# Router logits by column groups, and the mixing blocks as one product with a mask

## The chip, the cores and the metric

One core of one Trainium2 chip runs the whole layer as one program. The metric is the device time of an execution in microseconds (us). The core has a matrix engine (TensorE, PE in the rows; the loading of its stationary operand is PEld), a vector engine (VectorE, DVE), an activation engine (ScalarE, ACT), a general one (GpSimd, POOL), and a queue engine (SyncE, SP) that issues most DMAs. TensorE reads SBUF and writes PSUM (eight banks of 512 fp32 per partition). Each engine runs its instructions in order and waits on semaphores.

## The reference, cut to what matters

```python
# x: (64, 32, 512); cond: (64, 128)
h = gelu(cond @ W0 + b0); h = gelu(h @ W1 + b1)
att = softmax(h @ W2 + b2)                         # (64, 8)
agg_w = einsum('bk,koi->boi', att, weight)         # a 32x32 matrix for each batch row
agg_b = att @ bias_k
xt = einsum('boi,bih->boh', agg_w, x) + agg_b      # mixing; 2048 tokens of 512
logits = xt @ router_w + router_b                  # 512 -> 16 experts
scores = softmax(logits) + router_bias             # best 2 of 4 groups, best 2 experts in them
y = sum over experts of gate * ((silu(xt @ w1 + b1) * (xt @ w2 + b2)) @ w3 + b3)
z = (silu(xt @ sw1 + sb1) * (xt @ sw2 + sb2)) @ sw3 + sb3
out = x + y + z
```

## The kernel before

The 2048 tokens are 16 tiles of 128 (NT = 16), four tiles make a group of 512 columns (GT = 4, NG = 4), and a tile holds four batch rows of 32 channels (BPT = 4). The width of 512 is four chunks of 128 (C = 4).

**Start.** TensorE makes the conditioning in small products with warming products between them (`keep_warm`, products of the identity that nobody reads). The last, with `is_block`, puts `att` of every tile into PSUM bank 5, spread over partitions.

**Mixing stage.** VectorE's `mix(first, end)` builds the stationary matrices `mixT` of one or two tiles: it multiplies `mix_w` by `att` (L946), adds over the eight kernels (L972), copies the bias column (L974), and copies four 32x32 blocks per tile onto the diagonal of a zeroed 128x128 matrix in SBUF (L977, four copies of 32 partitions). Three calls stand at the start; later ones stand behind every second copy of a transposed tile. In step s of TensorE's loop (L605 to L631) stand the product that mixes tile s (512 columns, fp32), the four transposes of tile s-1 (L621), and the logits of tile s-2: four products with a 128x128 block of `xT` as the stationary operand and 16 columns of the router's weights as the moving one. An fp32 product is two instructions in the rows, a transpose is one. ScalarE evicts the mixed tile to a ring of four buffers (L825), from which SP stores it to HBM; VectorE copies the transposed tile to `xT` (L987). ScalarE and GpSimd split tiles into a rounded part and a rest (L835, L457).

**Behind it.** TensorE runs the first half of the shared expert (`shared_up`) without a break, while VectorE works on the routing from the logits: scores, the two best experts, `chosen`; then TensorE counts ranks with two products on `chosen` (`ranks_done`), VectorE makes slots and codes from them, and the dispatch product (32 products, `codes_ready`, `pool_codes`) makes the tables by which GpSimd gathers token rows. The experts' loop follows, then the shared expert's second half and the sums.

What sets the order is the program as written, engine by engine, with semaphores. Of importance below: `mix_copied` (VectorE to TensorE), `xt_ready` (ScalarE to TensorE and SP), `xT_ready` (VectorE to TensorE and ScalarE), `xt_stored` (a store has landed, ring buffer free), `logits_done` (TensorE to VectorE), `chosen_ready`, `ranks_done`.

## Time and profile before

| what | us |
|---|---|
| median of 3 runs | 261.38 |
| lowest and highest | 259.18, 262.07 |
| the profiled execution | 260.76 |
| its span, first to last instruction | 258.9 |
| mean granted TensorE clock, share of full | 0.993 |

The profiled execution is 1.86 us longer than its span. All times in the rows are from the span's start. In a row of the timeline stand: start, time from the first start to the last end, engine, line of the program, operation, out<-in, shapes, xcount, and in brackets the idle time before it with what ended it.

### The profile page before, as it was taken

To read this page: it belongs to the slowest core of one execution; us is meant where nothing else is said; L and a number is where in the kernel's file an instruction comes from. 1 tells how busy PE (TensorE), PEld (TensorE's weight loads), DVE (VectorE), ACT (ScalarE), POOL (GpSimd) and SP (SyncE) were. 2 spreads that over 40 slices of the span, in tenths; PEclk is the share of its full clock that TensorE was granted. 3 is DMA by queue.
4 is the path that set the end of the run, shared out by engine and by line. 5 is a ranking of instruction groups with operands and counts; after the bars stand their busy time and mean duration, and the time that the engine had idled before them with its cause. 6 is when DMAs were issued, how large, how long until landed. Compare 5 with 4: busy or idle time off the path is not lost.

```text
span 258.9 us, 4022 instructions
## 1 busy us (share of the span) xinstructions
PE 241.5 (93%) x1092; PEld 162.9 (63%) x1093; DVE 149.7 (58%) x314; ACT 78.7 (30%) x169; POOL 111.8 (43%) x135
## 2 busy tenths in 40 slices
PE   7847988999999889999999999999999999999695
PEld 6715756788875346667777777777777744444241
DVE  0599899649979977434333333333444401498982
ACT  2223535413147100333343333333333321111300
POOL 7782455410020344456666666666665321000720
PEclk9999999999999999999999999999999999999979
DMA  6998686697326938954555444455444224999853
GB/s 199 341 416 326 249 302 240 248 321 294 142 101 253 425 114 242 363 175 156 173 171 163 130 150 156 133 166 167 169 168 139 84 86 171 396 387 387 322 191 134
DMA packets 20699, 57.91 MB, mean 224 GB/s; under 512 B 2533, under 2 KB 2533, under 8 KB 20428
## 3 DMA queue, kind: packets, MB, share of 16 engines
q1 hardware_dynamic: 15084, 39.89, 42.2%
q0 software_dynamic: 5600, 17.83, 20.8%
q8 instruction: 7, 0.11, 0.2%
q14 instruction: 8, 0.07, 0.1%
HBM read 40.94 MB, written 17.30 MB: 225 GB/s over the span
## 4 chain that ended last, share of the span: by engine, by line
PE 81%; DVE 13%; DMA 3%; issue 2%; ACT 0%; DVEq 0%
PE psum L578 72%; PE psum L724 6%; DVE r L977 4%; DVE xT L1207 3%; DVE xT L972 2%; DVE xT L946 2%; DVE xT L987 2%; PE psum L621 2%; PE psum L737 2%; DMA late_region<-xt_rows,from_row 1%; DMA xT<-cond_pack 1%; DVE mix_bias L974 0%; ACT late_region L842 0%; DVE r L1163 0%; DVEq L1166 0%
## 5 line engine op out<-in xcount | busy, mean ns | idle before, releaser
L578 PE MATMUL psum<-wexp,r 128*128 x272 | 68.5, 381 | 0.3 <-DVE r L1163 0.2
L578 PEld LDWEIGHTS psum<-wexp,r 128*128 128x128 f32 x272 | 48.4, 190 | 22.8 <-issue 16.9
L946 DVE TENSOR_TENSOR r<-psum,ebias 128x256 f32<-128x256 f32 x34 | 14.4, 424 | 64.2 <-PE psum L578 64.2
L490 POOL DMA_INDIRECT late_region<-xt_rows,from_row x36 | 35.6, 990 | 23.9 <-issue 16.6
L496 POOL DMA_INDIRECT expert_rows<-late_region,to_row x33 | 33.3, 1010 | 26.8 <-issue 18.3
L578 PE MATMUL psum<-wexp,xt_sb 128*128 x68 | 34.8, 594 | 0.0
L883 ACT ACTIVATE r<-r 128x128 f32<-128x128 f32 x34 | 10.5, 310 | 57.6 <-DVE r L946 57.6
L578 PE MATMUL psum<-xT,shared_sb 128*128 128x512 f32 x64 | 28.0, 594 | 0.0
L889 ACT ACTIVATE late_region<-psum 128x512 f32<-128x512 f32 x34 | 20.3, 598 | 13.9 <-PE psum L578 13.9
L1163 DVE COPY r<-psum 128x512 f32<-128x512 f32 x36 | 24.5, 679 | 0.0
L724 PE MATMUL psum<-ident,late_region 128*128 128x128 f32 x144 | 21.6, 273 | 1.0 <-DMA late_region<-xt_rows,from_row 1.0
L578 PE MATMUL psum<-x_split,w_split 128*128 128x512 f32 x96 | 22.3, 392 | 0.0
L578 PEld LDWEIGHTS psum<-xT,shared_sb 128*128 128x128 f32 x64 | 12.0, 190 | 15.5 <-issue 14.6
L724 PEld LDWEIGHTS psum<-ident,late_region 128*128 128x128 f32 x144 | 17.9, 141 | 5.5 <-issue 2.0
L578 PEld LDWEIGHTS psum<-x_split,w_split 128*128 128x128 f32 x96 | 17.9, 188 | 3.7
L578 PE MATMUL psum<-router_sb,xT 128*128 128x16 f32 x128 | 15.8, 256 | 3.3 <-DVE xT L987 3.3
L825 ACT ACTIVATE xt_sb<-psum,mix_bias 128x512 f32<-128x512 f32 x16 | 11.0, 687 | 25.8 <-PE psum L578 15.8
L578 PEld LDWEIGHTS psum<-router_sb,xT 128*128 128x128 f32 x128 | 15.5, 192 | 4.1 <-DVE xT L987 4.0
L457 POOL TENSOR_TENSOR x_split<-xT,x_split 128x512 fp32r<-128x512 f32 x8 | 10.2, 1279 | 12.3 <-ACT x_split L835 12.3
L571 POOL TENSOR_TENSOR xt_sb<-xt_sb,wexp 128x512 f32<-128x512 f32 x2 | 3.3, 1663 | 27.1 <-ACT wexp L933 27.1
L987 DVE COPY xT<-psum 128x512 f32<-128x512 f32 x16 | 10.8, 689 | 5.8 <-PE psum L621 5.6
L879 ACT ACTIVATE xt_sb<-psum 128x128 f32<-128x128 f32 x34 | 9.4, 278 | 15.2 <-PE psum L737 15.2
(175 smaller groups left out, 311.0 us busy)
## 6 DMA issues: line engine op xcount, KB each, us to landing
wexp<-expert_pack SPq DMA_DIRECT2D x16, 768.0 KB, 5.3
wexp<-expert_rows SPq DMA_DIRECT2D x8, 1024.0 KB, 12.8
xt_rows<-xt_sb SPq DMA_DIRECT2D x16, 256.0 KB, 2.8
x_early<-x SPq DMA_DIRECT2D x2, 1024.0 KB, 8.1
late_region<-x SPq DMA_DIRECT2D x2, 1024.0 KB, 12.7
ebias<-expert_bias SPq DMA_DIRECT2D x1, 2048.0 KB, 7.1
out_dram<-x_early SPq DMA_DIRECT2D x8, 256.0 KB, 9.7
shared_sb<-shared_pack SPq DMA_DIRECT2D x1, 1536.0 KB, 16.4
```

Of the source, the lines that this page charges most:

```text
L457: T.tensor_tensor(rest, whole, part, ALU.subtract).then_inc(split_ready, 1)
L490: nc.gpsimd.indirect_dma_start(out=xg[:, slot, :], out_offset=None, in_=xt_dram[:, :], in_offset=bass.IndirectOffsetOnAxis(ap=index.bitcas ...
L496: nc.gpsimd.indirect_dma_start(out=y_dram[:, :], out_offset=bass.IndirectOffsetOnAxis(ap=index.bitcast(U32), axis=0), in_=y_sb[:, slot, :] ...
L578: return nc.tensor.matmul(dst, lhsT, rhs, start=start, stop=stop)
L724: last = nc.tensor.transpose(psum[:, b, c * P:(c + 1) * P], xg[:, slot, c * P:(c + 1) * P], ident[:, :])
L825: nc.scalar.activation(xt_ring[:, t % RING, :], psum[:, t % 2, :], ACT.Identity, bias=mix_bias[:, t:t + 1]).then_inc(xt_ready, 1)
L883: nc.scalar.activation(s_sb[:, b, :], h_sb[:, b, 0, :], ACT.Silu).then_inc(s_ready, 1)
L889: nc.scalar.activation(y_sb[:, slot, :], psum[:, 6 + b, :], ACT.Copy).then_inc(y_ready, 1)
L946: return nc.vector.tensor_tensor(dst, a, b, op)
L977: last = V.tensor_copy(mixT[rows, first:end, b * IN_C:(b + 1) * IN_C], mix_sum[rows, 0:T, 0:IN_C])
L987: V.tensor_copy(xT[:, t // GT, :, (t % GT) * P:(t % GT + 1) * P], psum[:, 2 + t % 2, :].rearrange("p (c n) -> p c n", c=C)).then_inc(xT_re ...
L1163: V.tensor_copy(xgT[:, b], psum[:, b, :].rearrange("p (c n) -> p c n", c=C)).then_inc(xgT_ready, 1)
```

## The change

Four edits, beside names.

1. **Block mask.** The four block copies and the bias copy in `mix` become one product: the summed rows, repeated four times along the free axis, times a mask of 128x4 that lies in PSUM bank 5 behind `att`. TensorE puts the mask there once, as identity times `in_block`; GpSimd makes `in_block` instead of zeroing `r1`. The sums live in a part of `wexp` that is loaded later, and ScalarE takes its bias from there.
2. **Logits by column groups.** Instead of 16 x 4 products with 16 moving columns there are, per group of four tiles, four products with 512 moving columns: chunk c of the router's weights (16 columns padded to 32 with zeros, `rw_wide`) is stationary in 32 columns of the array, and its result goes to partitions 32c to 32c+31 of one PSUM bank. ScalarE copies that bank to SBUF (`logits_copied`), and four products with `chunk_sum` (the identity folded to 16 columns, so that the four chunks are added) turn it back to token rows (`logits_to_rows`).
3. **Place of the last group.** The rows of the last group are made behind the first six products of `shared_up`, so `logits_done` comes there. SP's load of `ebias`, on whose space `rw_wide` and `chunk_sum` lie, now waits for `logits_done` too.
4. **Warming.** `keep_warm(8)` before the `is_block` product becomes `keep_warm(4)`.

TensorE's order in the mixing loop (in the names `x_early,r` is the mixing product, `ident,xt_sb` the transposes, `router_sb,xT` the logits). Before, steps 5 and 6:

```order
L578 MATMUL psum<-x_early,r 128x512 [waits xt_ready,mix_copied]
L621 MATMUL psum<-ident,xt_sb 128x128 [waits xT_ready,xt_ready]
L621 MATMUL psum<-ident,xt_sb 128x128 x3
L578 MATMUL psum<-router_sb,xT 128x16 [waits xT_ready]
L578 MATMUL psum<-router_sb,xT 128x16 x3
L578 MATMUL psum<-x_early,r 128x512 [waits xt_ready,mix_copied]
L621 MATMUL psum<-ident,xt_sb 128x128 [waits xT_ready,xt_ready]
L621 MATMUL psum<-ident,xt_sb 128x128 x3
L578 MATMUL psum<-router_sb,xT 128x16 [waits xT_ready]
L578 MATMUL psum<-router_sb,xT 128x16 x3
```

The same two steps now (`xT,ebias` are the column-group products, `ebias,r` the turning back):

```order
L590 MATMUL psum<-x_early,r 128x512 [waits xt_ready,mix_copied]
L651 MATMUL psum<-ident,xt_sb 128x128 [waits xT_ready,xt_ready]
L651 MATMUL psum<-ident,xt_sb 128x128 x3
L590 MATMUL psum<-xT,ebias 32x512 [waits rw_ready,xT_ready]
L590 MATMUL psum<-xT,ebias 32x512 x3
L590 MATMUL psum<-x_early,r 128x512 [waits xt_ready,mix_copied]
L651 MATMUL psum<-ident,xt_sb 128x128 [waits xT_ready,xt_ready]
L651 MATMUL psum<-ident,xt_sb 128x128 x3
L590 MATMUL psum<-ebias,r 128x16 [waits logitsT_ready]
L590 MATMUL psum<-ebias,r 128x16 x3
```

The two steps that follow hold no logits at all; the pattern repeats with steps 9 and 10, and 13 and 14.

VectorE, the mix of two tiles and the copies behind it, before:

```order
L946 TENSOR_TENSOR xT<-xT,psum 128x528
L972 TENSOR_REDUCE xT<-xT 128x66 [waits dve_chain]
L974 COPY mix_bias<-xT 128x2 [waits dve_chain]
L977 COPY r<-xT 32x2x32 x4
L987 COPY xT<-psum 128x4x128 [waits xtT_done] x2
```

And now:

```order
L980 TENSOR_TENSOR xT<-xT,psum 128x528
L1010 TENSOR_REDUCE wexp<-xT 128x66 [waits dve_chain]
L980 TENSOR_TENSOR r<-wexp,psum 128x256 [waits dve_chain]
L1024 COPY xT<-psum 128x4x128 [waits xtT_done] x2
```

Five copies became one product that reads the mask from PSUM; the copies of transposed tiles keep their places.

```diff
@@ -137,7 +137,6 @@
         mix_terms = early(P, 2 * KMIX * (IN_C + 1)).rearrange("p (t k o) -> p t k o", t=2, k=KMIX)
-        mix_sum = early(P, 2 * (IN_C + 1)).rearrange("p (t o) -> p t o", t=2)
         gateT = xT[0:GROWS, 0, :, :].rearrange("p c n -> p (c n)")[:, 0:TOKENS // 2].bitcast(BF16)
@@ -153,6 +152,10 @@
         wexp_flat = wexp[:, :, :].rearrange("p e n -> p (e n)")
+        mix_rows = wexp[:, E - 1, 0:NT * (IN_C + 1)].rearrange("p (t o) -> p t o", t=NT)
+        rw_wide = ebias_flat[:, 4 * DIM:4 * DIM + C * IN_C].rearrange("p (c e) -> p c e", c=C)
+        chunk_sum = ebias_flat[:, 4 * DIM + C * IN_C:4 * DIM + C * IN_C + E]
+        logitsT = [r1[:, q * GN:(q + 1) * GN] for q in (0, 1, 2, 1)]
         rows_k = wexp_flat[:, 0:NG * TOPK * GT * DIM].rearrange("p (g k t d) -> p g k t d", g=NG, k=TOPK, t=GT)
@@ -171,7 +174,7 @@
         sb12_sb = router_sb[:, C * E + 2 * E:].rearrange("p (w i) -> p w i", w=2)
-        mix_bias = sb("mix_bias", [P, NT])
+        in_block = sb("in_block", [P, BPT])
         rev_e = sb("rev_e", [P, E])
@@ -209,7 +212,7 @@
         masks_ready = sem("masks_ready")
-        blocks_zeroed = sem("blocks_zeroed")
+        in_block_ready = sem("in_block_ready")
         ident_bf_ready = sem("ident_bf_ready")
@@ -219,6 +222,9 @@
         mix_copied = sem("mix_copied")
+        rw_ready = sem("rw_ready")
+        logitsT_done = sem("logitsT_done")
+        logitsT_ready = sem("logitsT_ready")
         xt_done = sem("xt_done")
@@ -352,6 +358,7 @@
             sp.wait_ge(b3_ready, 1)
+            sp.wait_ge(logits_done, 1)
             sp.dma_start(ebias_flat, expert_bias.to_broadcast([P, E * 2 * INTER])).then_inc(half_loaded[0], 16)
@@ -404,7 +411,12 @@
                                     ).then_inc(masks_ready, 1)
-            nc.gpsimd.memset(r1[:, :], 0.0).then_inc(blocks_zeroed, 1)
+            link(nc.gpsimd.memset(in_block[:, :], 1.0))
+            link(nc.gpsimd.affine_select(out=in_block[:, :], in_=in_block[:, :], compare_op=ALU.is_ge, fill=0.0,
+                                         base=0, pattern=[[-IN_C, BPT]], channel_multiplier=1))
+            nc.gpsimd.affine_select(out=in_block[:, :], in_=in_block[:, :], compare_op=ALU.is_ge, fill=0.0,
+                                    base=IN_C - 1, pattern=[[IN_C, BPT]], channel_multiplier=-1
+                                    ).then_inc(in_block_ready, 1)
             link(nc.gpsimd.memset(ones_bf[:, :], 1.0))
@@ -593,14 +605,32 @@
             mm(psum[0:BS, 4, 0:KMIX], h2T, W2_sb).then_inc(pe_cond, 1)
-            keep_warm(8)
+            keep_warm(4)
             pe.wait_ge(masks_ready, 1)
             pe.wait_ge(dve_cond, 2)
             mm(psum[:, 5, 0:NT * KMIX], is_block.rearrange("b r i -> b (r i)"),
                att_spread.rearrange("b t k -> b (t k)")).then_inc(pe_cond, 1)
+            pe.wait_ge(in_block_ready, 1)
+            mm(psum[:, 5, NT * KMIX:NT * KMIX + BPT], ident[:, :], in_block[:, :]).then_inc(pe_cond, 1)
             keep_warm(8)
+
+            def logits_by_chunk(g):
+
+                if g == 0:
+                    pe.wait_ge(rw_ready, 1)
+                for c in range(C):
+                    last = mm(psum[c * IN_C:(c + 1) * IN_C, 6 + g % 2, :], rw_wide[:, c, :], xT[:, g, c, :])
+                last.then_inc(logitsT_done, 1)
+
+            def logits_to_rows(g):
+                pe.wait_ge(logitsT_ready, g + 1)
+                for t in range(g * GT, (g + 1) * GT):
+                    cols = slice((t % GT) * P, (t % GT + 1) * P)
+                    last = mm(psum[:, 4, t * E:(t + 1) * E], logitsT[g][:, cols], chunk_sum)
+                if g == NG - 1:
+                    last.then_inc(logits_done, 1)
@@ -621,15 +651,11 @@
                     last.then_inc(xtT_done, 1)
-                if s >= 2:
-                    t = s - 2
-                    if t == 0:
-                        pe.wait_ge(router_loaded, 16)
-                    pe.wait_ge(xT_ready, t + 1)
-                    for c in range(C):
-                        last = mm(psum[:, 4, t * E:(t + 1) * E], xT_tile(t, c), rw_sb[:, c, :],
-                                  start=(c == 0), stop=(c == C - 1))
-            last.then_inc(logits_done, 1)
+                if s >= GT + 1 and (s - 1) % GT == 0:
+                    pe.wait_ge(xT_ready, s - 1)
+                    logits_by_chunk(s // GT - 1)
+                if s >= GT + 2 and (s - 2) % GT == 0:
+                    logits_to_rows(s // GT - 1)
@@ -678,7 +704,7 @@
             pe.wait_ge(split_ready, SPLITS)
-            shared_up(0, 0)
+            shared_up(0, 0, between={(0, 1): lambda: logits_to_rows(NG - 1)})
             shared_up(0, 1)
@@ -816,6 +842,11 @@
             nc.scalar.activation(att_e, att, ACT.Exp, accum_out=att_sum).then_inc(act_cond, 1)
+
+            def logits_copied(g):
+                act.wait_ge(logitsT_done, g + 1)
+                nc.scalar.activation(logitsT[g], psum[:, 6 + g % 2, :], ACT.Copy).then_inc(logitsT_ready, 1)
+
             for t in range(NT):
@@ -823,7 +854,9 @@
                 nc.scalar.activation(xt_ring[:, t % RING, :], psum[:, t % 2, :], ACT.Identity,
-                                     bias=mix_bias[:, t:t + 1]).then_inc(xt_ready, 1)
+                                     bias=mix_rows[:, t, IN_C:IN_C + 1]).then_inc(xt_ready, 1)
+                if t >= GT + 1 and (t - 1) % GT == 0:
+                    logits_copied(t // GT - 1)
@@ -833,6 +866,7 @@
                     nc.scalar.activation(part, whole, ACT.Copy).then_inc(part_ready, 1)
+            logits_copied(NG - 1)
             act.wait_ge(shifted_ready, 1)
@@ -947,6 +981,9 @@
+            link(V.memset(rw_wide, 0.0))
+            dve.wait_ge(ident_ready, 1)
+            V.tensor_reduce(chunk_sum, ident[:, :].rearrange("p (c e) -> p e c", c=C)[:, 0:E, :], AX_X, ALU.add)
             dve.wait_ge(pe_cond, 3)
@@ -959,8 +996,9 @@
                                    op0=ALU.mult, op1=ALU.mult).then_inc(dve_cond, 1)
-            dve.wait_ge(pe_cond, 4)
-            dve.wait_ge(blocks_zeroed, 1)
+            dve.wait_ge(router_loaded, 16)
+            V.tensor_copy(rw_wide[:, :, 0:E], rw_sb).then_inc(rw_ready, 1)
+            dve.wait_ge(pe_cond, 5)
@@ -969,14 +1007,13 @@
                         att_here.unsqueeze(3).to_broadcast([P, T, KMIX, IN_C + 1]), ALU.mult))
-                link(V.tensor_reduce(mix_sum[:, 0:T], mix_terms[:, 0:T].rearrange("p t k o -> p t o k"),
+                link(V.tensor_reduce(mix_rows[:, first:end], mix_terms[:, 0:T].rearrange("p t k o -> p t o k"),
                                      AX_X, ALU.add))
-                V.tensor_copy(mix_bias[:, first:end], mix_sum[:, 0:T, IN_C])
-                for b in range(BPT):
-                    rows = slice(b * IN_C, (b + 1) * IN_C)
-                    last = V.tensor_copy(mixT[rows, first:end, b * IN_C:(b + 1) * IN_C],
-                                         mix_sum[rows, 0:T, 0:IN_C])
-                last.then_inc(mix_copied, 1)
+                shape = [P, T, BPT, IN_C]
+                tt(mixT[:, first:end].rearrange("p t (b o) -> p t b o", b=BPT),
+                   mix_rows[:, first:end, 0:IN_C].unsqueeze(2).to_broadcast(shape),
+                   psum[:, 5, NT * KMIX:NT * KMIX + BPT].unsqueeze(1).unsqueeze(3).to_broadcast(shape), ALU.mult
+                   ).then_inc(mix_copied, 1)
             for step in range(3):
                 mix(*MIXES[step])
```

## Rows read from the trace of the kernel before

**Rows 1.** The page: the chain that ended last by line, and one costly group.
```profile
PE psum L578 72%; PE psum L724 6%; DVE r L977 4%; DVE xT L1207 3%; DVE xT L972 2%; DVE xT L946 2%; DVE xT L987 2%; PE psum L621 2%; PE psum L737 2%; DMA late_region<-xt_rows,from_row 1%; DMA xT<-cond_pack 1%; DVE mix_bias L974 0%; ACT late_region L842 0%; DVE r L1163 0%; DVEq L1166 0%
...
L825 ACT ACTIVATE xt_sb<-psum,mix_bias 128x512 f32<-128x512 f32 x16 | 11.0, 687 | 25.8 <-PE psum L578 15.8
```
**Rows 2.** Stretches: length, PE, PEld, DVE, ACT, POOL busy, granted clock, DMA share, GB/s.
```profile
12.90:25.50 12.60, 7.33 (x36) 4.47 (x37) 12.10 (x25) 3.90 (x6) 6.99 (x8) 1.00 1.01 381
25.50:35.40 9.90, 9.04 (x59) 6.69 (x58) 8.90 (x19) 4.93 (x8) 5.12 (x5) 1.00 0.70 253
...
56.40:89.70 33.30, 33.15 (x141) 23.18 (x140) 29.51 (x63) 11.93 (x24) 4.41 (x6) 1.00 0.63 246
246.00:250.00 4.00, 3.97 (x6) 1.65 (x7) 4.00 (x7) 0.00 (x0) 1.51 (x2) 0.59 0.71 262
```
**Rows 3.** Timeline of TensorE, start and mixing stage.
```profile
7.47 0.38 PE L578 MATMUL psum<-xT 128*64 128x8 f32 x2
7.79 2.05 PE L578 MATMUL psum<-ident 128*128 128x128 f32 x16
9.77 0.48 PE L578 MATMUL psum<-xT 64*128 64x128 f32 x2
...
13.03 1.10 PE L578 MATMUL psum<-x_early,r 128*128 128x512 f32 x2 [0.80 <-DVE r L977]
...
19.29 1.12 PE L578 MATMUL psum<-x_early,r 128*128 128x512 f32 x2 [2.17 <-DVE r L977]
...
29.88 1.10 PE L578 MATMUL psum<-x_early,r 128*128 128x512 f32 x2
30.82 0.60 PE L621 MATMUL psum<-ident,xt_sb 128*128 128x128 f32 x4
31.26 0.96 PE L578 MATMUL psum<-router_sb,xT 128*128 128x16 f32 x8
...
34.48 1.06 PE L578 MATMUL psum<-router_sb,xT 128*128 128x16 f32 x8 [0.86 <-DVE xT L987]
```
**Rows 4.** Timeline of VectorE, mixes of one tile and of two.
```profile
9.06 0.35 DVE L959 SCALAR_TENSOR_TENSOR xT<-xT 64x128 f32<-64x128 f32 x1
10.29 0.43 DVE L946 TENSOR_TENSOR xT<-xT,psum 128x264 f32<-128x264 f32 x1 [0.89 <-PE psum L578]
10.76 0.63 DVE L972 TENSOR_REDUCE xT<-xT 128x33 f32<-128x264 f32 x1
...
15.54 0.70 DVE L946 TENSOR_TENSOR xT<-xT,psum 128x528 f32<-128x528 f32 x1
16.27 1.10 DVE L972 TENSOR_REDUCE xT<-xT 128x66 f32<-128x528 f32 x1
...
17.48 1.75 DVE L977 COPY r<-xT 32x64 f32<-32x64 f32 x4
19.27 0.69 DVE L987 COPY xT<-psum 128x512 f32<-128x512 f32 x1
...
27.12 0.78 DVE L977 COPY r<-xT 32x64 f32<-32x64 f32 x4
```
**Rows 5.** DMA issues between 14.9 and 15.5 us: KB, us to landing.
```profile
xt_rows<-xt_sb SPq DMA_DIRECT2D x1, 256.0 KB, 6.9
```
**Rows 6.** Timeline behind the mixing stage: TensorE, VectorE, GpSimd.
```profile
56.40 16.62 PE L578 MATMUL psum<-x_split,w_split 128*128 128x512 f32 x72
...
90.39 1.52 PE L578 MATMUL psum<-r,late_region 128*128 128x96 bf16 x32 [0.73 <-issue]
...
56.58 0.42 DVE L946 TENSOR_TENSOR late_region<-psum,router_sb 128x256 f32<-128x256 f32 x1 [1.16 <-PE psum L578]
...
73.29 0.42 DVE L1079 COPY late_region<-psum 128x256 f32<-128x256 f32 x1 [1.44 <-PE psum L578]
...
88.23 2.06 POOL L473 TENSOR_TENSOR r<-r,hi_code 128x480 bf16<-128x480 bf16 x1 [11.57 <-DVE r L1116]
```
**Rows 7.** Timeline of TensorE, the shared expert's second half.
```profile
211.14 25.05 PE L578 MATMUL psum<-xT,shared_sb 128*128 128x512 f32 x58
```

## The prediction

> **What bounds the kernel now.** I read the chain of waits first: TensorE's products end last, and the largest parts that are not TensorE are VectorE's block copies (L977) and the rest of the mix, all in the first 56 us [rows 1]. So the stretches come next. From 12.9 to 25.5 us VectorE is busy 12.10 of 12.60 us and TensorE 7.33: VectorE sets the pace. From 25.5 to 35.4, one group of four tiles, TensorE is busy 9.04 of 9.90 us and waits once, 0.86 us, for a copy of a transposed tile that stands behind a mix. From 56.4 to 89.7 TensorE is busy 33.15 of 33.30 [rows 2, 3]. The edits lie in the first two stretches; what they win or lose there is the time at which `shared_up` starts (S, now 56.40 [rows 6]), and what they add behind S counts by itself.
>
> **Start.** VectorE has `att_spread` at 9.41 (9.06 + 0.35 [rows 4]), but TensorE's product on it starts at 9.77, behind sixteen warming instructions from 7.79 on [rows 3]. Eight end near 8.8, so the product can start at 9.5; the mask's product adds some 0.2 behind it, and VectorE's first mix starts at 10.2 instead of 10.29. The copy of the router's weights on VectorE fits in its 0.89 us of idle time before that. The granted clock was 1.00, the 2.4 GHz level, through the 2.17 us in which TensorE waited before 19.29 [rows 2, 3], so I cost four fewer warming products at nothing.
>
> **The mix.** A product of VectorE with a PSUM operand took 0.43 us for 264 elements and 0.70 for 528, about 1.02 ns each; the block product of 256 is then 0.42, of 128 0.29. It takes the place of four copies in 1.75 us (0.78 in some mixes) and a bias copy [rows 4]. A mix of two tiles becomes 0.70 + 1.10 + 0.42 and gaps = 2.32 us, of one tile 1.46. From 10.2 the three first mixes end at 11.66, 13.12 and 15.44; the third mixing product, now at 19.29 [rows 3], can start at 15.5: **3.8 us won early**. Most of that reaches the first column-group products. They wait for VectorE's copy of tile 3 (15.44 + 0.72 + 2.32 + 1.32 + 2.32 + 0.69 = 22.8), and for the transposes of tile 4, whose eviction needs the store of tile 0. That store, issued at 14.9, lands 6.9 us later, at 21.8 [rows 5], behind loads in the same queue, and an earlier issue does not change that; with the eviction (0.69 [rows 1]) and the transposes TensorE is at 23.06.
>
> **The logits.** A mixing product with its transposes takes 1.38 us from start to start (29.88 to 31.26), eight instructions of old logits 0.81 (0.96 less the 0.15 by which the shown ends lag) [rows 3]. Call c the time of the four column-group products of a group. The turning back is again eight instructions with 16 columns, 0.81. A period is then four times 1.38, c, 0.81, and a wait: VectorE's copy of tile 6 starts 0.66 behind its transposes, a mix and the copy of tile 7 follow, so that copy ends 0.66 + 0.72 + 2.32 + 0.69 = 4.39 later, where TensorE is ready after 3.19; with the semaphore 1.26 us. Period 7.59 + c, against 9.90 now: even at c = 2.3. The last stretch has two mixing products, three sets of transposes, one turning back and waits of 1.5 us: 5.51 + c. So S = 23.06 + 2 x 7.59 + 5.51 + 4c = 43.75 + 4c. The same walk over the kernel before gives 55.95 where the trace has 56.40, so I add 0.45: **S = 44.2 + 4c**.
>
> ScalarE gains four copies of 512 columns (0.69 as its evictions [rows 1]), hidden: TensorE needs each only behind a mixing product and a set of transposes (1.38 us), or behind six products (1.4). GpSimd loses the zeroing and gains three small operations, off the path.
>
> **The value of c.** No row shows column groups. A 512-column fp32 product is two instructions of 0.43 us (25.05 us for 58 [rows 7]). If nothing overlaps, c = 8 x 0.43 = 3.44; if all four columns run side by side, 0.86. I take the middle case. The two instructions of one product use the same 32 columns and cannot overlap each other; instructions start in the order of the program; so each product's second half runs beside the next one's first: five slots, 2.15 us. Going to narrow columns and back costs something: the 128x64 product took 0.32 us to the next start for a pair, where a full-width pair of 16 columns takes 0.20, and the 64x128 pair took 0.48, where a full-width pair of 128 columns takes 2.05 / 8 = 0.26 [rows 3]; bounds 0 and 0.35, I take 0.25 since going in is partly hidden in the 1.26 us wait. **c = 2.4.** The Trainium skill speaks against free switching: TensorEngine Tiling (Array Packing), Key Properties, says that a change of the tiling mode drains the engine. The rows on the two odd-shaped products agree in sign, and the sum has the 0.25 either way.
>
> **Behind S.** The last turning back now stands in `shared_up`: +0.81 on TensorE. `logits_done` comes 1.39 (six products) + 0.81 + 0.15 = 2.35 us behind S, where VectorE now starts 0.18 behind it. VectorE's later start of 2.17 is covered as far as the counts: it waits 1.44 us there for TensorE, and TensorE comes 0.81 later itself, 2.25 in all [rows 6]. From there on both are 0.81 late, and the dispatch (which starts 90.39, when GpSimd's codes end at 88.23 + 2.06 [rows 6]) follows. The load of `ebias` starts some 2 us later behind S; its reader stands beyond 100 us. I count 0.9.
>
> **Sum.** 44.2 + 4c - 56.4 + 0.9 = 4c - 11.3; with c = 2.4, -1.7 us. The profiled execution took 260.76, so **259.1 us**. That execution is 0.62 below the median of the runs shown, 261.38. Without switching cost -2.7 (258.1), with 0.35 -1.3 (259.5).
>
> **Rival 1: all four columns overlap.** c = 0.86 + 0.25 = 1.1, net -6.9, **253.9 us**. For it: four different parts of the array and of PSUM, and only one semaphore per group. Against: the order of the halves above, which no row can prove. The Trainium skill, TensorE: Matmul & The Clock Gate, Part 3 (Packing small matmuls), reports 2.38 times for three column tiles and starts a few ns apart; its span rule would give this case. The same part says that products start and end strictly in order, by which the second half of each would hold up the next, as I forecast. No run here shows it yet.
>
> **Rival 2: the column groups run one after another** (slower). Where each fp32 product streams 512 columns alone, c = 3.44 + 0.25 = 3.7, net +3.5, **264.3 us**. Place: TensorE at the end of each group; it decides from c = 2.83 on, where the sum is zero. For it: every 512-column product in the trace goes at 0.43 per instruction, whatever its content, and the old form needed 3.26 per group. Against: the output partitions put each product into its own 32 columns.
>
> **Rival 3: the routing starts too late.** Cover for `logits_done` is 2.25 against 2.17 needed. If ScalarE's last copy or the turning back comes 1 to 2 us later than worked out, VectorE's routing and the dispatch are late by that, and the result is 260 to 261.5, no change.
>
> Worth noting for any outcome: by the same walk the mask alone, with the old logits, would put S at 49.1, 7.3 earlier. The column groups pay only if c is near 1; at c = 2.4 they give back over four us of what the mask wins.
>
> **Numbers.** Chances: forecast 0.50, rival 1 0.15, rival 2 0.23, rival 3 0.12. About 1%, 2.6 us, can be told from no change; the three runs before spread by 2.9. Part of that may be the clock: behind a wait near 246 us the granted clock was 0.59 on average over 4 us [rows 2], between the two levels, and a shift of the whole end can move that by up to 1.8 us either way. Faster by over 1%: rival 1, and 0.4 of the forecast (low c, or the clock): 0.36 with a little of rival 3. Slower by over 1%: most of rival 2, and 0.04 of mishaps in the routing: 0.20. Within 1%: 0.44. The range reaches from rival 1 to just short of rival 2: 253.3 to 264.0; the forecast's own is 258.0 to 260.0.
>
> **What the profile after would show.** Right: the third mixing product near 15.5; one VectorE product of 0.42 us per pair of tiles and no 32-row copies; the first column-group products near 23; 2.4 us from the first of four to the next mixing product; `shared_up` near 53.8; the dispatch 34.9 us behind that. Wrong: starts of the four products 0.9 apart (rival 2) or all within a short time (rival 1), a VectorE wait that no longer stands before the counts (rival 3), or a block product that takes as long as the copies did.

## The result and the profile after

The changed kernel took **250.95 us** (median of 4 runs, 250.71 to 251.96) beside 260.56 us for the kernel before on the same chip: a ratio of 0.965 [0.961, 0.970]. The prediction was 259.1 with a range from 253.3 to 264.0, so it was wrong: right in sign, far too small. The profiled execution took 250.74 us, its span is 249.0, the granted clock 0.991. Medians here are over all executions of a kernel; a ratio leaves out those over 1.5% above their kernel's fastest, among them one of 489.55 us of the kernel with all stores first and one of 418.35 us of the kernel before.

Where the two profiled executions stand at the same points (us from the span's start):

| point | before | after | difference |
|---|---|---|---|
| third mixing product | 19.29 | 14.78 | -4.51 |
| `shared_up` begins (S) | 56.40 | 49.38 | -7.02 |
| dispatch begins | 90.39 | 84.32 | -6.07 |
| second half of the shared expert begins | 207.52 | 200.97 | -6.55 |
| last product of TensorE ends | 255.70 | 245.44 | -10.26 |
| span | 258.9 | 249.0 | -9.9 |

So there are two gains, some 6 to 7 us in the mixing stage and 3.7 us in the last 48 us. The second was in no term of the prediction's sum.

The page's chain of waits, which answers to [rows 1]: the block copies are gone from it, and the store of a tile (`xt_rows<-xt_sb`, 4% of the span) is new.
```profile
PE psum L590 69%; PE psum L750 6%; DMA xt_rows<-xt_sb 4%; DVE xT L1244 3%; DVE xT L980 2%; PE psum L651 2%; PE psum L763 2%; DVE xT L1024 1%; DMA xT<-cond_pack 1%; DVE xt_sb L1244 1%; DVE x_early L980 1%; DVE wexp L1010 1%; ACT xt_sb L856 1%; DVE xt_sb L980 1%; ACT L844 1%
```
The timeline of VectorE, where the first mixes were in [rows 4]: product, sum, and now one block product with a PSUM operand, 0.29 us for a tile and 0.42 for two.
```profile
9.79 0.43 DVE L980 TENSOR_TENSOR xT<-xT,psum 128x264 f32<-128x264 f32 x1 [0.85 <-PE psum L590]
10.25 0.63 DVE L1010 TENSOR_REDUCE wexp<-xT 128x33 f32<-128x264 f32 x1
10.92 0.29 DVE L980 TENSOR_TENSOR r<-wexp,psum 128x128 f32<-128x128 f32 x1
...
12.44 0.70 DVE L980 TENSOR_TENSOR xT<-xT,psum 128x528 f32<-128x528 f32 x1
13.17 1.10 DVE L1010 TENSOR_REDUCE wexp<-xT 128x66 f32<-128x528 f32 x1
14.31 0.42 DVE L980 TENSOR_TENSOR r<-wexp,psum 128x256 f32<-128x256 f32 x1
```
The timeline of TensorE, beside [rows 3]. `psum<-xT,ebias` with 128*32 are the four column products of a group (eight instructions); the number in brackets is the wait before them.
```profile
14.78 1.13 PE L590 MATMUL psum<-x_early,r 128*128 128x512 f32 x2 [0.64 <-DVE r L980]
...
19.03 1.02 PE L590 MATMUL psum<-x_early,r 128*128 128x512 f32 x2
23.11 1.12 PE L651 MATMUL psum<-ident,xt_sb 128*128 128x128 f32 x4 [3.05 <-ACT xt_sb L856]
24.15 1.94 PE L590 MATMUL psum<-xT,ebias 128*32 128x512 f32 x8
26.02 1.19 PE L590 MATMUL psum<-x_early,r 128*128 128x512 f32 x2
...
33.44 1.06 PE L590 MATMUL psum<-xT,ebias 128*32 128x512 f32 x8 [1.01 <-DVE xT L1024]
34.44 1.12 PE L590 MATMUL psum<-late_region,r 128*128 128x512 f32 x2
...
49.38 1.67 PE L590 MATMUL psum<-x_split,w_split 128*128 128x512 f32 x6
```
From start to next start a group's four products take 1.00 us (33.44 to 34.44), where the prediction had 2.4. The first group took 1.87, and the four transposes ahead of it 1.04 instead of some 0.5. The stretches around them, columns as in [rows 2], show why: the granted clock was 0.50, the 1.2 GHz level, behind the 3.05 us in which TensorE waited.
```profile
19.00:24.00 5.00, 1.95 (x8) 0.94 (x6) 2.49 (x4) 1.63 (x3) 2.93 (x4) 0.88 1.00 403
24.00:26.00 2.00, 2.00 (x10) 0.20 (x8) 1.70 (x3) 0.15 (x1) 0.92 (x1) 0.50 1.03 421
```
That wait comes from a store. ScalarE's timeline shows that its eviction of tile 4 waited for the store of tile 0 to land, and the issue row of that store gives 8.9 us where [rows 5] had 6.9. SP issued it at 13.31, before at 14.94: so it landed at 22.2 and before at 21.8, nearly the same time in spite of the earlier issue.
```profile
22.37 0.69 ACT L856 ACTIVATE xt_sb<-psum,wexp 128x512 f32<-128x512 f32 x1 [3.54 <-DMA xt_rows<-xt_sb]
```
```profile
xt_rows<-xt_sb SPq DMA_DIRECT2D x1, 256.0 KB, 8.9
```
How eight instructions fit into 1.00 us is read by cutting the timeline: up to 33.88 TensorE has begun four of the eight, and all eight have begun by 33.92.
```profile
33.44 0.64 PE L590 MATMUL psum<-xT,ebias 128*32 128x512 f32 x4 [1.01 <-DVE xT L1024]
```
So four halves begin together at 33.44 and the other four 0.45 us later: two slots, not five. The rows do not name the columns; that the first four are the first halves of the four products is argued, since the two halves of one product use the same columns.

**The end.** GpSimd adds the four tiles of the last group; VectorE's additions of the third group (L1207 before, L1244 after) have two operands in SBUF. Before, GpSimd starts just ahead of VectorE's last two: these take some 1.75 us each instead of 0.74, all eight 7.53 us, and TensorE waits 2.08 us and then runs slowly. The timelines of before, of GpSimd, VectorE and TensorE:
```profile
241.32 3.29 POOL L571 TENSOR_TENSOR xt_sb<-xt_sb,wexp 128x512 f32<-128x512 f32 x2 [27.05 <-ACT wexp L933]
...
237.63 7.53 DVE L1207 SCALAR_TENSOR_TENSOR xT<-wexp,tops,xT 128x512 f32<-128x512 f32 x8
...
246.03 3.08 PE L578 MATMUL psum<-shared_sb,late_region 128*128 128x512 f32 x4 [2.08 <-DVE xT L946]
248.90 0.63 PE L578 MATMUL psum<-xt_sb,xT 102*128 102x512 bf16 x1
```
The summary of VectorE's line in that stretch (ns: least, median, most):
```profile
L1207 DVE SCALAR_TENSOR_TENSOR xT<-wexp,tops,xT x8: 743/744/1762, 237.6 to 243.4; 128x512 f32<-128x512 f32 x8
```
The same timelines of after: the eight are done in 5.51 us (by 236.6) when GpSimd has just begun; the additions that it slows are those of the last group (3.38 us for two), for which nobody waits. TensorE has no wait there.
```profile
236.05 2.91 POOL L583 TENSOR_TENSOR xt_sb<-xt_sb,wexp 128x512 f32<-128x512 f32 x2 [28.33 <-ACT wexp L967]
...
231.09 5.51 DVE L1244 SCALAR_TENSOR_TENSOR xT<-wexp,tops,xT 128x512 f32<-128x512 f32 x8
...
239.03 3.38 DVE L1244 SCALAR_TENSOR_TENSOR xt_sb<-wexp,tops,xt_sb 128x512 f32<-128x512 f32 x2
...
237.46 1.96 PE L590 MATMUL psum<-shared_sb,late_region 128*128 128x512 f32 x4
```
Both kernels begin the eight 30.1 us after the second shared half; GpSimd begins 33.8 us after it before and 35.1 after. By the program it starts when ScalarE has scaled the last rows that were loaded, so 1.3 us in that step decide over 3.7 us.

### The profile page after: what moved, and what is told of

Read it like the earlier page. It is cut to its first block, busy times and chain, and to the rows that moved or that the text cites. A ratio compares the mean times of both kernels' runs of the same rounds, so it can differ in the third digit from the quotient of the medians.

```text
span 249.0 us, 3856 instructions
## 1 busy us (share of the span) xinstructions
PE 233.3 (94%) x1022; PEld 151.1 (61%) x1023; DVE 138.9 (56%) x281; ACT 80.7 (32%) x173; POOL 109.8 (44%) x137
## 4 chain that ended last, share of the span: by engine, by line
PE 78%; DVE 12%; DMA 5%; issue 2%; ACT 2%; DVEq 0%; ACTq 0%
PE psum L590 69%; PE psum L750 6%; DMA xt_rows<-xt_sb 4%; DVE xT L1244 3%; DVE xT L980 2%; PE psum L651 2%; PE psum L763 2%; DVE xT L1024 1%; DMA xT<-cond_pack 1%; DVE xt_sb L1244 1%; DVE x_early L980 1%; DVE wexp L1010 1%; ACT xt_sb L856 1%; DVE xt_sb L980 1%; ACT L844 1%
## 5 line engine op out<-in xcount | busy, mean ns | idle before, releaser
L1024 DVE COPY xT<-psum 128x512 f32<-128x512 f32 x16 | 10.7, 686 | 10.1 <-PE psum L651 10.1
L856 ACT ACTIVATE xt_sb<-psum,wexp 128x512 f32<-128x512 f32 x16 | 11.0, 686 | 13.9 <-DVE r L980 4.3
L651 PEld LDWEIGHTS psum<-ident,xt_sb 128*128 128x128 f32 x64 | 8.1, 145 | 11.9 <-ACT xt_sb L856 6.7
L469 POOL TENSOR_TENSOR x_split<-xT,x_split 128x512 fp32r<-128x512 f32 x8 | 10.1, 1271 | 7.9 <-ACT x_split L868 7.8
L651 PE MATMUL psum<-ident,xt_sb 128*128 128x128 f32 x64 | 10.2, 284 | 3.4 <-ACT xt_sb L856 3.4
```

The costliest lines, as they stand in the source:

```text
L469: T.tensor_tensor(rest, whole, part, ALU.subtract).then_inc(split_ready, 1)
L651: last = nc.tensor.transpose(psum[:, 2 + t % 2, c * P:(c + 1) * P], xt_ring[:, t % RING, c * P:(c + 1) * P], ident[:, :])
L856: nc.scalar.activation(xt_ring[:, t % RING, :], psum[:, t % 2, :], ACT.Identity, bias=mix_rows[:, t, IN_C:IN_C + 1]).then_inc(xt_ready, 1)
L1024: V.tensor_copy(xT[:, t // GT, :, (t % GT) * P:(t % GT + 1) * P], psum[:, 2 + t % 2, :].rearrange("p (c n) -> p c n", c=C)).then_inc(xT_re ...
```

## The experiments

Below, "front" is S, and "end" the time from the first product of the second shared half to the last product of TensorE (48.18 us before, 44.47 after). Times are medians, ratios are to the kernel before on the same chip. The experiments ran on three chips, on which the kernel before took 261.36, 261.33 and 260.62 us, so differences of less than 1 us between their medians say nothing. The edits are cut to their main lines and stand against the changed kernel where nothing else is said.

### One part at a time

**The mask alone**: edits 1 and 4, with the old logits.
```diff
-                    last = mm(psum[c * IN_C:(c + 1) * IN_C, 6 + g % 2, :], rw_wide[:, c, :], xT[:, g, c, :])
+                    last = mm(psum[:, 4, t * E:(t + 1) * E], xT_tile(t, c), rw_sb[:, c, :],
+                              start=(c == 0), stop=(c == C - 1))
```


> The kernel before with the block mask and the shorter warming, old logits. Theory A (the walk of the prediction): the shared expert starts near 49.1 us in the trace, 7.3 earlier than before and about as early as in the changed kernel (49.4), and the 0.95 us that the turned-back rows add behind it are not there; so the dispatch product starts near 83.1, 1.2 us earlier than in the changed kernel, and the time is 249.5 us if the last stretch runs as in the changed kernel, 253 if as before. Rival B (the column groups bring most of the gain): about 257.


Measured: 252.66 us, ratio 0.967 [0.960, 0.974]. S at 49.86 and the dispatch at 83.87, 0.45 us earlier than in the whole change, though this execution began badly: sixteen warming instructions took 3.29 us and not 2.03, and the first product of x stood at 14.16 instead of 11.47. The granted clock is shown as 1.00 there, so that row does not show this slowness. The end was 48.17 us with a wait of 2.09: GpSimd again met the third group (34.2 us behind the second shared half).
```profile
11.03 3.29 PE L583 MATMUL psum<-ident 128*128 128x128 f32 x16
14.16 1.88 PE L583 MATMUL psum<-x_early,r 128*128 128x512 f32 x4
...
49.86 0.49 PE L583 MATMUL psum<-x_split,w_split 128*128 128x512 f32 x1
...
239.00 3.63 PE L583 MATMUL psum<-shared_sb,late_region 128*128 128x512 f32 x4 [2.09 <-DVE xT L953]
```
So the mask carries the front by itself.

**The column groups alone**: edits 2 and 3, with the old mix.
```diff
-                tt(mixT[:, first:end].rearrange("p t (b o) -> p t b o", b=BPT), ...
+                V.tensor_copy(mix_bias[:, first:end], mix_sum[:, 0:T, IN_C])
+                for b in range(BPT): ... last = V.tensor_copy(mixT[rows, first:end, ...], ...)
```


> The changed kernel with the old block copies and the longer warming. Theory A: VectorE's mix still sets the pace, so the column groups hardly help: shared expert from about 55, dispatch 0.5 us earlier than before, 258 to 260 us. Rival B: about 254.


Measured: 260.66 us, ratio 1.000 [0.993, 1.007]; S at 58.05, 1.65 later than before. TensorE waits 2.54 us ahead of the first two groups, and 2.40 ahead of the third, for VectorE's copies, which stand behind the block copies.
```profile
29.09 1.07 PE L585 MATMUL psum<-xT,ebias 128*32 128x512 f32 x8 [2.54 <-DVE xT L1019]
...
39.84 1.06 PE L585 MATMUL psum<-xT,ebias 128*32 128x512 f32 x8 [2.54 <-DVE xT L1019]
```
A period of 10.75 us, where the kernel before has 9.90: what the columns save on TensorE is not where this stage waits. The end here was 44.48 without the mask, with GpSimd 35.0 us behind the second shared half, so the front's loss and the end's gain nearly cancel.

**The column products at full width**, so that they cannot lie side by side: each chunk's 16 columns stand in their own place of a 128-column matrix, and the four products add into one bank.
```diff
-                    last = mm(psum[c * IN_C:(c + 1) * IN_C, 6 + g % 2, :], rw_wide[:, c, :], xT[:, g, c, :])
+                    last = mm(psum[:, 6 + g % 2, :], rw_wide[:, c, :], xT[:, g, c, :],
+                              start=(c == 0), stop=(c == C - 1))
```


> The changed kernel, but the four products of a group use stationary operands of 128 columns (the router's chunk c in columns 32c to 32c+15, the rest zeros) and add up in one PSUM bank: the same logits, no column groups. Theory A (the groups' overlap is what made the four products 1.0 us): they take 8 x 0.43 = 3.4 us, and the time is 4 x 2.4 = 9.8 us above the changed kernel, 260 to 262 us. Rival C (the wide moving operand alone is what helps): as the changed kernel, 251.


Measured: 260.30 us, S at 58.16. A group's products take 3.53 us (35.20 to 38.73) instead of 1.00.
```profile
35.20 3.70 PE L590 MATMUL psum<-xT,ebias 128*128 128x512 f32 x8 [1.02 <-DVE xT L1027]
38.73 1.02 PE L590 MATMUL psum<-late_region,r 128*128 128x512 f32 x2
```
Four times 2.53 is 10.1 us; S is 8.8 later and the second shared half 9.1. The overlap of the columns is shown as the reason for c = 1.0.

### The wait before tile 4

**The shared weights' load behind the store of tile 3** on SP's queue.
```diff
-            sp.dma_start(shared_sb[:, :], shared_pack).then_inc(shared_loaded, 16)
...
+                if t == 3:
+                    sp.dma_start(shared_sb[:, :], shared_pack).then_inc(shared_loaded, 16)
```


> The changed kernel with the load of the shared weights (1.5 MB) issued behind the store of tile 3 instead of ahead of all stores. Theory A: TensorE's wait of 3.05 us ahead of the transposes of tile 4 is for the store of tile 0, which stands behind that load in the queue; without it the wait falls below 0.7 us, the clock stays at 2.4 GHz, the first column-group products take 1.0 us instead of 1.87, and the time falls by 3 us to 247.5 to 248.5. Rival D (VectorE would hold TensorE there anyway): less than 1 us.


Measured: 252.24 us (249.01 to 253.15), ratio 0.959 [0.949, 0.968], S at 49.91: no gain that is clear of the spread. The wait at tile 4 is gone (first group at 22.29, 1.0 us long), but the same wait stands at tile 8, again with the second group at the 1.2 GHz level behind it (granted clock 0.50 from 31.8 to 33.8).
```profile
31.09 0.69 ACT L857 ACTIVATE xt_sb<-psum,wexp 128x512 f32<-128x512 f32 x1 [3.20 <-DMA xt_rows<-xt_sb]
...
31.84 1.11 PE L652 MATMUL psum<-ident,xt_sb 128*128 128x128 f32 x4 [2.64 <-ACT xt_sb L857]
32.88 1.94 PE L591 MATMUL psum<-xT,ebias 128*32 128x512 f32 x8
```
One load out of the way was not enough: the next store stood behind the moved load and an expert load.

**All stores ahead of the bulk loads**: as above, and the eight expert loads behind the sixteen stores.
```diff
-                if t % 2 == 1:
-                    place = HALF + t // 2
-                    sp.dma_start(wexp[:, place, :], expert_pack[place]).then_inc(half_loaded[0], 16)
+            for place in range(HALF, E):
+                sp.dma_start(wexp[:, place, :], expert_pack[place]).then_inc(half_loaded[0], 16)
```


> The changed kernel with the shared weights' load behind the store of tile 3 and all eight expert loads behind the sixteen stores on SP's queue. Theory A (the 3 us wait of TensorE before tile 4, and the same wait before tile 8 where only the shared load was moved, come from stores that land behind the bulk loads of the one queue): no wait over 1.5 us on TensorE between 12 and 46, no first product of four columns at half clock, shared products from about 46 instead of 49.4, total about 247.5. Theory B (the eviction's four buffers or ScalarE limit the stage, the loads do not): shared products from 49 or later and a total of 250 to 252; also if the late expert loads delay the first expert products, 250 or more with the shared products early.


Measured: 248.34 us, ratio 0.955 [0.945, 0.965], an interval that just meets that of the changed kernel; S at 45.66, 3.72 sooner than in the changed kernel, and the second shared half 3.66 sooner. No wait of TensorE in this stage is over 1.15 us.
```profile
21.36 1.06 PE L590 MATMUL psum<-xT,ebias 128*32 128x512 f32 x8 [1.15 <-DVE xT L1024]
...
45.66 1.67 PE L590 MATMUL psum<-x_split,w_split 128*128 128x512 f32 x6
```

**Eight warming products again.**
```diff
-            keep_warm(4)
+            keep_warm(8)
             pe.wait_ge(masks_ready, 1)
```


> The changed kernel with eight instead of four warming products ahead of the mask product, as before. Theory A (these products lie in TensorE's idle time, as the prediction had it): first product of x within 0.5 us of 11.5, third mixing product within 0.3 us of 14.8, total within 1 us of the changed kernel's 250.95. Theory B (fewer warming products are part of the gain): the first x product 0.5 to 2.7 us later, as in the mask-only kernel (14.2), and the total 1 to 2 us above.


Measured: 248.97 us, 2.0 under the changed kernel's median, though the ratio, 0.960 [0.951, 0.969], overlaps that kernel's. Neither theory as written. The third mixing product stands 1.01 us later, at 15.79, but the four products account for only some 0.2 of that. In the changed kernel TensorE's product on `att_spread` waits for VectorE and starts 0.15 us behind it (8.98); here it comes without a wait, 0.36 us behind VectorE (9.96 against 9.60). The other 0.8 were lost ahead of these products; two kernels with four of them had the third mixing product nearly as late (15.43 with the shared load moved, 15.30 in the last but one below). TensorE's timeline in the changed kernel:
```profile
8.98 0.46 PE L590 MATMUL psum<-xT 64*128 64x128 f32 x2 [0.88 <-DVE xT L996]
```
And in this one:
```profile
9.96 0.48 PE L590 MATMUL psum<-xT 64*128 64x128 f32 x2
...
22.69 0.66 PE L651 MATMUL psum<-ident,xt_sb 128*128 128x128 f32 x4 [1.64 <-ACT xt_sb L856]
23.28 1.07 PE L590 MATMUL psum<-xT,ebias 128*32 128x512 f32 x8
```
The store of tile 0, issued at 14.32, took 7.5 us and landed at 21.8 once more. TensorE waited 1.64 us at tile 4 and not 3.05, the first group ran at full clock, and S was 47.59. What this is worth shows beside the changed kernel run again (the last experiment): there the store landed at 21.8 as well and the transposes of tile 4 start at 22.78, 0.09 later than here, but behind a wait of 2.77 us and at half clock, and S is 1.64 later. So some 1.5 us of S are the clock's and not the landing's. All ten executions of the changed kernel have a mean granted clock of 0.991 to 0.993; of the four here three have 0.999 or 1.000 (248.82 to 249.00 us) and one 0.993 (251.24). A later start before a fixed landing costs nothing here, and behind the shorter wait the clock held; whether the four products are what made that so is not shown.

### The end

**GpSimd's additions held**, in the kernel before, until VectorE has summed the first tile of the third group.
```diff
             pool.wait_ge(x_again_loaded, 16 * (NT - EARLY * GT))
+            pool.wait_ge(z_ready, LAST * GT - GT + 1)
```


> The kernel before with one more wait: GpSimd begins the four additions of the last group only when VectorE has summed the first tile of the third group (z_ready at 9), so that none of them lies beside VectorE's two-operand additions of the third group (L1207). Theory A (3.4 of the 9.6 us of the change come from the end of the kernel: beside GpSimd's addition VectorE's addition takes 1.75 us instead of 0.74, TensorE then waits 2.08 us and runs at half clock): the front stays as before (second shared half from about 207.5 in the span), from there to the last product 44.5 instead of 48.2 us, TensorE without the 2 us wait, total about 257.0. Theory B (the 3.4 us belong to the changed front or to chance, GpSimd's place costs nothing): 48 us again from there and a total of 260 to 261.5.


Measured: 259.52 us, ratio 0.993 [0.988, 0.997]. The end is 44.46 us and TensorE has no wait there, with GpSimd at 245.81, after VectorE's eight additions (5.51 us again).
```profile
239.44 5.51 DVE L1208 SCALAR_TENSOR_TENSOR xT<-wexp,tops,xT 128x512 f32<-128x512 f32 x8
...
245.81 2.50 POOL L572 TENSOR_TENSOR xt_sb<-xt_sb,wexp 128x512 f32<-128x512 f32 x2 [29.73 <-DVE xT L947]
...
245.81 1.96 PE L579 MATMUL psum<-shared_sb,late_region 128*128 128x512 f32 x4
```
Mechanism A holds in the profile, but the time falls by 0.7% only, 1.9 us, not 3.7. S was 58.24 in this execution, 1.84 later than before with nothing changed there; the granted clock from 13 to 25 us was 0.72 in it and 1.00 in the profile of before.

**The kernel before, not edited**, to see what varies.


> The kernel before, not edited, once more with a profile. GpSimd's wait gave the kernel before 1.8 us in the median of twelve runs where its profile promised 3.7. Theory A (GpSimd's last additions meet VectorE's third group in a part of the executions only, as the last rows land): this execution may show 44.5 or 48.2 us from the second shared half to the last product; 44.5 would show that the meeting is not a property of the kernel. Theory B (they meet in every execution, and the wait costs something elsewhere): 48.2 again, with GpSimd's addition 33.5 to 34.5 us behind the second shared half.


One execution, 263.65 us. GpSimd met VectorE again (34.1 us behind the second shared half) and TensorE waited 2.08 us again, but its clock stayed at the 2.4 GHz level (1.00 from 250 to 258): the end took 46.48 us. In the mixing stage, however, behind a wait of 2.63 us, the products ran at half speed (0.50 from 22 to 25), the stretch from 13 to 25 us had a granted clock of 0.86, and S came at 60.98.
```profile
20.70 1.21 PE L578 MATMUL psum<-x_early,r 128*128 128x512 f32 x2 [2.63 <-DVE r L977]
21.70 1.06 PE L621 MATMUL psum<-ident,xt_sb 128*128 128x128 f32 x4
...
250.62 1.96 PE L578 MATMUL psum<-shared_sb,late_region 128*128 128x512 f32 x4 [2.08 <-DVE xT L946]
252.41 0.38 PE L578 MATMUL psum<-xt_sb,xT 102*128 102x512 bf16 x1
```
Neither theory as written. The collision stood in both profiles of before; it costs 2.0 us by itself (46.48 against 44.46), and 1.7 more where the clock falls behind it. That fits the 1.9 us of the times, but two profiles do not give a frequency. The times hint that not every execution pays: four of the kernel before with a mean granted clock of 1.000 took 257.89 to 258.50 us, three with GpSimd's wait and the same clock 257.71 to 258.32. No profile shows such an execution of the kernel before.

**The mask alone with the same wait of GpSimd** (added to the mask alone).
```diff
+            pool.wait_ge(z_ready, LAST * GT - GT + 1)
```


> The block mask alone (router logits in rows of one tile, as before) with the same wait of GpSimd. Theory A (mask and the end of the kernel are all of the gain, the column groups add nothing): second shared half from 200.5, 44.5 us to the last product, total about 249.0, a little under the changed kernel's 250.95. Theory B (the column groups carry part of the gain): no faster than the mask alone, 252 to 253.


Measured: 250.54 us, ratio 0.965 [0.958, 0.971], with S at 48.12 and an end of 44.46. The whole change has 0.965 too. So the mask with a free end gives as much as the whole change, and the column groups, as the change places them, add nothing in the front that these runs can tell. But they are what frees the end: in all eight profiles of kernels with edits 2 and 3 ScalarE begins to scale the last rows 34.1 to 34.6 us behind the second shared half, in the six without them 32.9 to 33.4. Which part of these edits makes the rows land later is open. The expected 249.0 was 1.5 too low: over the mask alone GpSimd's wait won 2.1 us by the medians and 0.6 by the ratios, whose intervals overlap, where its profile gave 3.7.

### What the column groups are worth

**Mask alone, GpSimd's wait, stores first**: only the column groups are missing of the kernel with 248.34 (which needed no wait of GpSimd, its end was 44.46).


> The block mask with the old logits, GpSimd's wait, and the stores ahead of the shared and expert loads as in the kernel of 248.34: column groups are all that is missing of it. Theory A (in the mask-only kernel TensorE has no break between 15 and 48 us, 2.19 us a tile, so earlier stores give it nothing; the column groups leave TensorE room that only earlier stores let it use): shared products from 48 again, total 250 to 251, so the column groups are worth some 2 us once the stores are early. Theory B (the order of the queue alone carries the 2.6 us, column groups are worth nothing in any order): shared products from about 45.7, total about 248.


Measured: 250.56 us, S at 48.34. TensorE is busy all 8.00 us of this stretch, so earlier stores have nothing to give.
```profile
32.00:40.00 8.00, 8.00 (x54) 6.18 (x53) 6.74 (x10) 4.69 (x8) 4.33 (x5) 1.00 0.28 102
```
The column groups are worth 2.2 us in the medians, 1.9 by the ratios (0.962 [0.957, 0.968] here, whose interval overlaps that of 0.955), and 2.7 in S, of which 0.95 goes again behind S for the rows turned back, once the stores are early: the old logits fill TensorE, the new ones leave room that only then is used. Part of the difference of the medians may be the clock. In the profiled execution it was 0.51 to 0.56 from 48.3 to 52 us, although TensorE had not waited since 15.3; three of the six executions have a mean of 0.993 like this one (251.19 to 251.30 us), the others 0.996 to 1.000 (248.92 to 249.93).

**All edits (stores first, GpSimd's wait), and the products of groups 1 to 3 one tile later**, where VectorE's copies are done.
```diff
-                if s >= GT + 1 and (s - 1) % GT == 0:
+                if s == NT + 1: ...
+                elif s >= GT + 2 and (s - 2) % GT == 0:
```


> The changed kernel with three edits at once: the stores ahead of the shared and expert loads, GpSimd's wait at the end, and in groups 1 to 3 the column products one tile later, so that VectorE's copy of the group's fourth tile is done before TensorE comes to them. Theory A (the 0.3 to 1.2 us that TensorE still waits before each of those three groups goes away, and nothing else takes its place): shared products from 43.5 to 44.5 in place of 45.66, total 246 to 247.5. Theory B (VectorE's copies set the pace of the stage, the wait moves to the next transposes or products): shared products from 45.3 to 46, total about 248.3 as with the stores alone.


Measured: **246.99 us**, ratio 0.950 [0.944, 0.955], 4 us under the changed kernel on the same chip (250.94, below): theory A, and the fastest kernel of all these. S at 43.19, and the waits ahead of the first three groups are gone.
```profile
23.02 1.06 PE L591 MATMUL psum<-xT,ebias 128*32 128x512 f32 x8
...
30.29 1.07 PE L591 MATMUL psum<-xT,ebias 128*32 128x512 f32 x8
...
43.19 1.66 PE L591 MATMUL psum<-x_split,w_split 128*128 128x512 f32 x6
```

**The changed kernel, not edited.**


> The changed kernel, not edited, once more beside these. Theory A (start of GpSimd's addition after VectorE's third group is a property of this kernel): 44.5 us from the second shared half to the last product, TensorE's wait before tile 4 between 1.6 and 3.1 us as the first store lands, total 250.3 to 251.5. Theory B (it is luck of the last rows' landing): 48 us there, a total of 253 to 254.5 in this run.


Measured: 250.94 us. S at 49.23, wait before tile 4 2.77 us with the first group at half speed behind it (1.86 us to the next product), end 44.46: theory A.
```profile
22.78 1.08 PE L651 MATMUL psum<-ident,xt_sb 128*128 128x128 f32 x4 [2.77 <-ACT xt_sb L856]
23.79 1.93 PE L590 MATMUL psum<-xT,ebias 128*32 128x512 f32 x8
```

## Why the prediction was wrong

- **Start and mix: right.** The first mix stood at 9.79 (10.2 predicted), the third mixing product at 14.78 (15.5), the block product took 0.42, as worked out from [rows 4].
- **The value of c: the step that failed.** The prediction had "instructions start in the order of the program; so each product's second half runs beside the next one's first: five slots". In the trace four of the eight instructions begin together and the other four 0.45 us later, so the step is two slots, 0.86, and the 0.14 left bounds the change of width, where 0.25 was taken. (The 0.25 leaned on a pair with 64 columns, 0.32 us to the next start; in the profile of after that pair takes 0.21, a full-width pair 0.20. And the 0.48 of the other pair is a shown end; to the next start it is 0.41.) Measured c was 1.00 and not 2.4, which is 5.6 of the 8.3 us by which the forecast missed. With 1.00 in its sum the prediction gives 44.2 + 4.0 - 56.4 + 0.9 = -7.3, **253.5 us**: rival 1, with its 253.9, was the case that happened. The Trainium skill, TensorE: Matmul & The Clock Gate, Part 3, gave rival 1 its span rule; by it, as an estimate, two spans of little over 0.43 us make 0.9, and the runs come near that: 1.00, against 3.53 at full width. The words of the same part of the Trainium skill on strictly ordered starts, on which the forecast leaned, do not lead to the five slots here.
- **First column products at 23.06: 1.09 too early.** That an earlier issue does not bring the store of tile 0 in sooner was right: it landed at 22.2, and 21.8 was taken. The transposes so began at 23.11 and not 22.49. The rest is the clock behind the wait of 3.05 us, which no term had: the transposes took 1.04 us and not 0.57, and the first group then 0.87 more than the others. This is why S was 49.38 and not 48.2. The stores-first run shows the loads in the queue as the cause of the wait: without them ahead S is 3.7 us sooner.
- **"Four fewer warming products at nothing".** On the path the sum had them, at 0.27 us (9.5 for 9.77), and 0.2 is what the run with eight shows. What was put at nothing is the clock; there the run with eight kept the clock in three of four executions behind a shorter wait, 2 us faster. That the four products are the reason is not shown.
- **Behind S +0.9: right.** The dispatch stands 34.94 us behind S (33.99 before). VectorE has the logits at 51.89, 2.51 behind S (2.35 predicted). From the dispatch to the second shared half 0.48 us more were won; what wins them is not settled.
- **The end: missing.** The prediction had only clock luck of 1.8 us behind the wait near 246 in [rows 2], and did not ask where that wait came from. It came from GpSimd beside VectorE: 2.0 us by itself, 3.7 with the clock. That the change moved the two apart was luck: no edit aimed at it, and it came with the column groups and not with the mask. The Trainium skill, SBUF — State Buffer, Who interferes with whom, says that a VectorE instruction with two SBUF inputs contends with a GpSimd one that reads SBUF: 0.74 against 1.76 us here, while VectorE's sums with a PSUM operand beside the same additions (four in 2.48 us in both kernels' profiles) were not slower.
- **"The mask alone would put S at 49.1": right**, 48.1 to 49.9 in three runs. That column groups pay "only if c is near 1" was too kind: with c at 1.0 they paid nothing in the front until the stores came out of their way.

From -7.3: front +1.2, expert loop -0.5, end -3.7, and +0.4 behind the last product, together -9.9; measured -10.0. For the medians one reservation stays: an execution of before varies in S by up to 4.6 us and in the end by 1.7, so the split of the 9.6 us into mask and end (some 7 to 9 and 0.6 to 2) is known to about 1 us.

## What to carry to other kernels

A wait in the profile before is a term of the sum even where the change doesn't touch its place: ask what made it, since a change elsewhere may move two engines apart or together. When a stage gets faster, look at what has a fixed time of its own, here stores behind bulk loads in one queue; the gain ends there, and a longer wait may cost the clock as well. And price a new form of instruction by its likeliest mechanism with both ends as cases: a middle case without a row behind it had half of the chances here and did not come out.

## What was not expected of the hardware

- An fp32 product of two instructions in each of four column groups: four of the eight instructions begin within 0.03 us, the other four 0.45 us later. Four products take 1.00 us where full-width ones take 3.53.
- The same wait of 2.08 us was followed by half clock in one execution of a kernel and by full clock in another; and with the mask and early stores the granted clock fell to 0.51 at 48.3 us though TensorE had not waited since 15.3.
- In two executions warming products took 3.29 and 2.99 us for sixteen instructions instead of 2.03 in stretches whose granted clock is shown as 1.00 (the mask alone, and the kernel before with GpSimd's wait).
